# First 24 gathers of a graph layer from x, multiplied by W on TensorE, beside the making of x W

## The chip, the cores and the metric

The kernel runs on one core of a Trainium2 chip. The metric is the device time of one execution in microseconds (us); the time before is the median of three runs. The profile shows one of these executions. Its engines are TensorE (PE in the rows, PEld for its weight loads), VectorE (DVE), ScalarE (ACT), GpSimd (POOL) and SyncE (SP). SP, ACT and GpSimd issue DMAs; a row such as `SPq` or `ACTq` is the issue of one.

## The reference

Four graph layers run one after the other on 6250 nodes of 128 features, each followed by a layer norm. The graph has 206,250 edges, sorted by destination. The change touches layer 0 alone: every edge takes the row of x W at its source, times a row made from 16 edge attributes, and the sum over the edges of a destination is added to x.

```python
def _L0_gnn_ref(x, edge_index, edge_attr, W, edge_w, b):
    src, dst = (edge_index[0], edge_index[1])
    xw = x @ W
    ew = edge_attr @ edge_w
    msg = xw[src] * ew
    out = jax.ops.segment_sum(msg, dst, num_segments=x.shape[0])
    return out + b
...
x = _layernorm(x + _L0_gnn_ref(x, edge_index, edge_attr_16, L0_gnn_W, L0_gnn_edge_w, L0_gnn_b), axis=-1)
```

Layers 1 to 3 sum over the same edges without edge attributes; the kernel does that with a dense matrix of counts (the adjacency), which it makes while layer 0 runs.

## The kernel before

**Prologue.** TensorE multiplies the transposed x by W in seven turns of seven blocks of 128 nodes (L1377). ScalarE copies each turn out of the accumulators in two pieces (L1681) into one of four rooms, which lie in the memory that the gathered rows use later, and SyncE stores the room to `xw` in memory (L645). From the fifth turn on the copy waits until the room's last store has ended. Beside that VectorE finds where the edges of each pair of nodes begin: 25 reductions (L838), then the bias is copied into all of `yT` (L842) and the edges' places in their windows are made (L844). GpSimd makes constants, and one small gather (L749) that needs VectorE's first result.

**The loop** has 202 steps (n) of 1024 edges. In a step:

- GpSimd issues eight gathers (L775), each of 128 rows of `xw` of 512 bytes, 64 KB. There are four rooms for the gathered rows, so step n waits for the messages of step n - 4. From step 7 on the fifth gather waits as well for the window of step n - 2 (`s_pe`) and for the adjacency tiles made up to then (`s_amm`).
- TensorE makes the edge rows one step ahead ("edge products", L1386). VectorE multiplies them by the gathered rows as soon as all eight have landed: the message, two instructions (L984). TensorE sums the messages into a window of 64 nodes by a product with a 0/1 matrix (L1465), and VectorE adds the window to `yT` (L902).
- From step 5 on one or two tiles of the adjacency are made in a step: VectorE makes 0/1 matrices (L888, L890), TensorE multiplies them in two halves (L1438), ScalarE copies each half out (L1696), and SyncE stores the tile (L661). The edges for it come in 25 further gathers ("slots", L758), which VectorE splits in step 2 for the first time.
- From step 15 on some steps also take a job of the layers' next parts; the first of these reads x, which ScalarE loads by two DMAs (L1686, L1687), issued after the last store of x W has ended.

**After the loop** come the layers 1 to 3, mostly dense matrix products on TensorE. They start from the summed `yT`.

What sets the order: every engine runs the order in which its code is written, and waits at semaphores. On GpSimd the wait ahead of the first gather (`pool.wait_ge` on `s_in["src"]`, `s_rowxw` and `s_rowst`) is for all source numbers and for all stores of x W. On SyncE the loads at the start stand in a row: the first table, W, four pieces of the transposed x, the other weights, the source numbers, and so on.

## Time and profile before

| | |
|---|---|
| median of three runs | 2810.82 us (2810.70 to 2816.72) |
| the profiled execution | 2810.70 us, span 2808.9 us |
| TensorE busy | 2238.8 us, 80% of the span |
| VectorE busy | 1564.6 us, 56% |
| GpSimd busy | 1651.5 us, 59% |
| ScalarE busy | 498.4 us, 18% |
| TensorE's granted clock, mean | 0.809 |

Busy times are sums over stages that are limited by different things: the prologue to 32 us, the loop to about 2100 us, the dense layers behind it. In the timeline a row gives the start in us from the span's start, the duration in us, the engine, the line of the kernel, the operation, what it writes and reads, how many instructions are merged in the row (xN), and in brackets the engine's idle time ahead of it with what ended it. TensorE's clock has two levels, 1.2 and 2.4 GHz; the column PEclk shows 0.50 and 1.00 for them.

### The profile page before, as it was taken

The numbers are of one execution on the slowest core, as the hardware profiler recorded it, in microseconds if no ns is written. First come the engines' busy times: TensorE is split into PE (matmuls) and PEld (weight loads), VectorE is DVE, ScalarE is ACT, GpSimd is POOL, SyncE is SP. The second block draws the span as 40 slices with busy tenths as digits, with TensorE's granted clock in tenths as the row PEclk, the third lists the DMA queues.
The fourth block names the chain that finished last, engine by engine and source line by source line (L and its number), as shares of the span: only waits on it lengthen the run. The fifth ranks groups of instructions, "written<-read, shape, count | busy, mean of one in ns | idle before, by whom it ended". The sixth has DMA issues, their size and how long they took to land.

```text
span 2808.9 us, 35420 instructions
## 1 busy us (share of the span) xinstructions
PE 2238.8 (80%) x13074; PEld 1423.0 (51%) x13074; DVE 1564.6 (56%) x2590; ACT 498.4 (18%) x798; POOL 1651.5 (59%) x1762
## 2 busy tenths in 40 slices
PE   4677777886787767787778787777778999999995
PEld 3455555554554545555555554544444444455553
DVE  3688888788887666666667664222228111212126
ACT  1122222222222111111212111000004111111113
POOL 4777777777777777777777777777762000012222
PEclk6566777778787777787878777777679999999998
DMA  7234443445455444554545557544447787776651
GB/s 231 82 110 127 124 136 123 137 142 141 140 153 153 125 141 127 143 148 129 168 141 154 153 152 145 152 127 112 100 124 245 261 290 276 259 287 247 246 200 46
DMA packets 456701, 456.24 MB, mean 162 GB/s; under 512 B 204789, under 2 KB 402250, under 8 KB 456522
## 3 DMA queue, kind: packets, MB, share of 16 engines
q1 hardware_dynamic: 212046, 271.95, 28.3%
q0 software_dynamic: 52832, 109.16, 14.7%
q10 hardware_dynamic: 191644, 72.77, 10.6%
q8 instruction: 109, 1.79, 0.3%
q14 instruction: 70, 0.57, 0.1%
HBM read 368.61 MB, written 85.13 MB: 162 GB/s over the span
## 4 chain that ended last, share of the span: by engine, by line
PE 45%; POOL 20%; issue 11%; DMA 11%; DVE 10%; ACT 1%; DVEq 1%; SPq 1%; POOLq 0%; ACTq 0%
POOL big L775 19%; PE pb L1465 11%; DMA big<-xw,big 10%; PE pb L1569 9%; PE pb L1570 9%; PE pb L1386 6%; DVE big L984 4%; PE pb L1438 3%; PE pb L1428 2%; PE pb L1444 2%; DVE big L888 2%; DVE big L890 1%; PE pb L1587 1%; DVEq L897 1%; ACT tmp L1696 1%
## 5 line engine op out<-in xcount | busy, mean ns | idle before, releaser
L775 POOL DMA_INDIRECT big<-xw,big x1612 | 1525.8, 947 | 528.8 <-issue 496.0
L1386 PE MATMUL pb<-big 64*128 64x512 f32 x808 | 310.1, 853 | 463.1 <-DVE big L984 460.0
L984 DVE TENSOR_TENSOR big<-pb,big 128x512 f32<-128x512 f32 x404 | 259.8, 685 | 702.6 <-DMA big<-xw,big 679.7
L1465 PEld LDWEIGHTS pb<-big 128*128 128x128 f32 x3232 | 539.5, 261 | 219.0 <-issue 170.7
L1465 PE MATMUL pb<-big 128*128 128x64 f32 x3232 | 572.5, 351 | 1.4 <-DVE big L984 1.4
L1696 ACT CAST tmp<-pb 128x784 f16<-128x784 f32 x392 | 318.3, 812 | 1310.0 <-PE pb L1438 1275.5
L888 DVE TENSOR_TENSOR big<-pb,big 128x2048 f16<-128x2048 f32 x196 | 447.1, 2281 | 0.8
L890 DVE TENSOR_TENSOR big<-pb,big 128x1568 f16<-128x1568 f32 x196 | 348.4, 1778 | 0.0
L1386 PEld LDWEIGHTS pb<-big 64*128 64x128 f32 x808 | 77.1, 233 | 502.2 <-DVE big L984 490.7
L1438 PE MATMUL pb<-big 128*128 128x98 f16 x3136 | 249.0, 232 | 45.4 <-ACT tmp L1696 28.9
L1438 PEld LDWEIGHTS pb<-big 128*128 128x128 f16 x3136 | 222.0, 117 | 106.1 <-issue 47.7
L1569 PE MATMUL pb<-big,x 128*128 128x512 f16 (+1 forms) x637 | 229.7, 369 | 6.5 <-issue 6.5
L1569 PE MATMUL pb<-big,yT 128*128 128x512 f16 (+1 forms) x637 | 230.2, 368 | 3.8 <-DMA big<-at 3.8
L1570 PE MATMUL pb<-big,yT 128*128 128x512 f16 (+1 forms) x637 | 230.2, 368 | 0.0
L1570 PE MATMUL pb<-big,x 128*128 128x512 f16 (+1 forms) x637 | 229.4, 368 | 0.0
L1428 PE MATMUL pb<-big,yT 128*128 128x448 f16 x910 | 219.2, 398 | 0.0
L1444 PE MATMUL pb<-tmp,ident 128*128 128x392 f16 x784 | 215.6, 411 | 0.0
L802 POOL TENSOR_TENSOR wts<-x 128x256 f32<-128x256 f32 x24 | 16.8, 723 | 246.5 <-DVE x L1266 246.5
L790 POOL MEMSET vecs<- 128x256 f32 x1 | 0.3, 312 | 271.0 <-DVE yT L1213 271.0
L1428 PEld LDWEIGHTS pb<-big,yT 128*128 128x128 f16 x910 | 101.4, 113 | 102.0 <-issue 44.5
L855 DVE TENSOR_TENSOR big<-pb,big 128x512 f32<-128x512 f32 x202 | 137.2, 679 | 0.0
L1194 DVE SCALAR_TENSOR_TENSOR y<-pb,small,y 128x128 f32<-128x128 f32 x49 | 13.9, 344 | 182.8 <-PE pb L1587 182.8
(230 smaller groups left out, 1639.7 us busy)
## 6 DMA issues: line engine op xcount, KB each, us to landing
at<-tmp SPq DMA_DIRECT2D x196, 392.0 KB
big<-at SPq DMA_DIRECT2D x24, 3200.0 KB, 11.2
big<-at SPq DMA_DIRECT2D x24, 3072.0 KB, 19.8
big<-xw,big POOLq DMA_INDIRECT x1612
big<-at ACTq DMA_DIRECT2D x22, 896.0 KB
big<-at ACTq DMA_DIRECT2D x27, 672.0 KB
big<-in_ea SPq DMA_DIRECT2D x202, 64.0 KB
tmp<-at ACTq DMA_DIRECT2D x9, 896.0 KB
```

The source lines that it names most:

```text
L775: nc.gpsimd.indirect_dma_start(gath[:, T8 * (n % NG) + t % T8, :], None, xw_d, bass.IndirectOffsetOnAxis(ap=src_i[:, t:t + 1], axis=0)).th ...
L888: nc.vector.tensor_tensor(hot_lo[:, at_pair:at_pair + NPR, :], cols[:, 0:P].unsqueeze(1).broadcast_to([P, NPR, P]), lokeyT[:, b % 3, c:c + ...
L890: last = nc.vector.tensor_tensor(hot_key[:, at_pair:at_pair + NPR, :], cols[:, P:P + KW].unsqueeze(1).broadcast_to([P, NPR, KW]), lokeyT[: ...
L984: nc.vector.tensor_tensor(msg[:, T8 * (n % 2) + 4 * q:T8 * (n % 2) + 4 * q + 4, :], PB[:, q, :].rearrange("p (t f) -> p t f", f=D), gath[: ...
L1386: last = nc.tensor.matmul(PB[:, q, :], ea[4 * ED * q:4 * ED * q + 4 * ED, n % NG, :], edge_w[4 * ED * q:4 * ED * q + 4 * ED, 4 * q:4 * q + ...
L1428: nc.tensor.matmul(bank, parts_v[part_of][:, b0 + b, :], a_piece[:, :, b, :], start=(b == 0 and part_of == 0), stop=(b == size - 1 and par ...
L1438: last = nc.tensor.matmul(PB[:, 4 + g, i * KW:i * KW + KW], hot_lo[:, at_pair, :], hot_key[:, at_pair, :], start=True, stop=True)
L1444: last = nc.tensor.matmul(PB[:, 6, 0:NB * T8], ident16[:, :], stage[:, j % 2, :].rearrange("p (h d) -> p h d", d=SN)[:, :, g * T8:g * T8 + ...
L1465: last = nc.tensor.matmul(PB[:, 2 + n % 2, 0:WIN], msg[:, T8 * (n % 2) + t, :], hot_win[:, T8 * (n % 2) + t, :], start=(t == 0), stop=(t = ...
L1569: nc.tensor.matmul(PB[:, c, 0:n], hi[:, b, :], piece, start=(b == 0), stop=False)
L1570: last = nc.tensor.matmul(PB[:, c, 0:n], lo[:, b, :], piece, start=False, stop=(k == 2 and b == NB - 1))
L1696: nc.scalar.copy(stage[:, j % 2, :].rearrange("p (h d) -> p h d", d=SN)[:, :, c:c + 4 * GP].rearrange("p h (k i a) -> p h k i a", k=2, a=2 ...
```

## The change

Three steps of eight gathers (KX = 3) take rows of the input x instead of rows of `xw`. They need only the first 24 columns of the source numbers, which come by a DMA of their own, second in SyncE's row. The waits for all of x W and for the other source numbers move from the first gather to the first gather of step 3; the first slot gather moves from behind step 0 to behind step 2. TensorE turns the gathered rows (`turned_rows`, four tiles of 128 rows at a time), ScalarE copies the turned rows out, TensorE multiplies them by W (`rows_w`), and ScalarE copies the product back over the gathered rows; there are six such groups, all ahead of the first edge product. x W for the other steps is staged in the memory of the messages and of the adjacency's 0/1 matrices, since the gathered rows' memory is in use. VectorE waits for all stores of x W before its first message. ScalarE's load of x stands behind its new copies.

The diff, cut to what the steps need:

```diff
@@ -442,7 +445,21 @@
         POOL_ALL = 2 + 6 * 2 * NPAIR
         aggr_at, shift_at = [], []
         xT = y_room[:, 0:NB, :].rearrange("p b f -> p (b f)")
-        xwS = gath
+        key_rows = hot_key.rearrange("p t f -> p (t f)")
+        xw_rooms = [msg[:, T8 * t:T8 * t + BT, :] for t in range(2)]
+        xw_rooms += [key_rows[:, t * 2 * BT * D:(t + 1) * 2 * BT * D].bitcast(F32).rearrange("p (t f) -> p t f", f=D) for t in range(2)]
+
+        def turn_at(k):
+
+            return k + 1 if k < 2 else 2 * k
+
+        def product_at(k):
+
+            return min(2 * k + 3, 4 * KX)
+
+        turned_at = ring_at + 2 * 2 * T
+        turned_rooms = [BIG[:, turned_at + k * 2 * 4 * P:turned_at + (k + 1) * 2 * 4 * P].bitcast(F32) for k in range(2)]
+        assert turned_at + 4 * 4 * P <= 2 * CH * NB * SN
 
 
 
@@ -623,6 +640,8 @@
         @block.sync
         def _(sp):
             sp.dma_start(firstq_i, firstq_d.broadcast_to([P, QN])).then_inc(s_in["firsts"], 16)
+            with nc.allow_non_contiguous_dma(reason="24 columns, once"):
+                sp.dma_start(src_i[:, 0:KX * T8], src_d[:, 0:KX * T8]).then_inc(s_src0, 16)
             sp.dma_start(wts[:, W_L0, :], w_d[W_L0]).then_inc(s_in["w0"], 16)
             for part_of in range(4):
                 c0, c1 = XT_CUTS[part_of] * BT * P, XT_CUTS[part_of + 1] * BT * P
@@ -630,7 +649,7 @@
             sp.dma_start(wts[:, 1:7, :], w_d[1:7].rearrange("w k n -> k w n")).then_inc(s_in["w"], 16)
             with nc.allow_non_contiguous_dma(reason="128 numbers, once"):
                 sp.dma_start(bias_l0[:, :], vec_d[0, B_L0, :].rearrange("(f o) -> f o", o=1)).then_inc(s_in["w"], 16)
-            sp.dma_start(src_i, src_d).then_inc(s_in["src"], 16)
+            sp.dma_start(src_i[:, KX * T8:T], src_d[:, KX * T8:T]).then_inc(s_in["src"], 16)
             sp.dma_start(half_i, half_d.broadcast_to([P, NH])).then_inc(s_in["edges"], 16)
             sp.dma_start(dst_i, dst_d).then_inc(s_in["edges"], 16)
             sp.dma_start(win_tab[:, :], half_d).then_inc(s_in["edges"], 16)
@@ -643,7 +662,7 @@
             for t in range(NT):
                 sp.wait_ge(s_rowev, 2 * t + 2)
                 sp.dma_start(xw_d[t * BT * P:(t + 1) * BT * P, :].rearrange("(b p) f -> p b f", p=P),
-                             xwS[:, T8 * (t % 4):T8 * (t % 4) + BT, :]).then_inc(s_rowst[t % 4], 16)
+                             xw_rooms[t % 4]).then_inc(s_rowst[t % 4], 16)
                 if t == NT - 2:
                     sp.wait_ge(s_first, 2)
                     sp.dma_start(first_d.rearrange("(p b) o -> p (b o)", b=NPB), run_edge[:, :]).then_inc(s_run, 16)
@@ -758,12 +777,15 @@
                 nc.gpsimd.indirect_dma_start(slots[:, b % 2, :, :].rearrange("p e k -> p (e k)"), None, edges_d,
                                              bass.IndirectOffsetOnAxis(ap=first_edge[:, b:b + 1], axis=0)).then_inc(s_slot[b % 2], 16)
 
-            pool.wait_ge(s_in["src"], 16)
-            pool.wait_ge(s_rowxw, 2 * NT)
-            for h in range(4):
-                pool.wait_ge(s_rowst[h], 16 * ((NT + 3 - h) // 4))
+            pool.wait_ge(s_src0, 16)
             pool.sem_inc(s_seen, 1)
             for n in range(NH):
+                if n == KX:
+                    pool.wait_ge(s_in["src"], 16)
+                    pool.wait_ge(s_rowxw, 2 * NT)
+                    for h in range(4):
+                        pool.wait_ge(s_rowst[h], 16 * ((NT + 3 - h) // 4))
+                    pool.sem_inc(s_seen, 1)
                 if n >= NG:
                     pool.wait_ge(s_msg, 2 * (n - NG) + 2)
                     pool.sem_inc(s_seen, 1)
@@ -772,9 +794,9 @@
                         pool.wait_ge(s_pe, n)
                         pool.wait_ge(s_amm, 2 * made_by(n - 2))
                         pool.sem_inc(s_seen, 1)
-                    nc.gpsimd.indirect_dma_start(gath[:, T8 * (n % NG) + t % T8, :], None, xw_d,
+                    nc.gpsimd.indirect_dma_start(gath[:, T8 * (n % NG) + t % T8, :], None, x_d if n < KX else xw_d,
                                                  bass.IndirectOffsetOnAxis(ap=src_i[:, t:t + 1], axis=0)).then_inc(s_gath[n % NG], 16)
-                if n == 0:
+                if n == KX - 1:
                     slots_in(0)
                 if n + 6 in SLOTS_AT:
                     slots_in(SLOTS_AT[n + 6])
@@ -977,10 +999,15 @@
                 v.wait_ge(s_deg["col"], 4 * turn + 4)
 
             window_hot(0)
+            for h in range(4):
+                v.wait_ge(s_rowst[h], 16 * ((NT + 3 - h) // 4))
             for n in range(NH):
                 v.wait_ge(s_pe, n + 1)
-                v.wait_ge(s_gath[n % NG], 16 * T8 * (n // NG) + 16 * min(T8, ET - n * T8))
+                if n >= KX:
+                    v.wait_ge(s_gath[n % NG], 16 * T8 * (n // NG) + 16 * min(T8, ET - n * T8))
                 for q in range(2):
+                    if n < KX:
+                        v.wait_ge(s_first_act, product_at(2 * n + q))
                     nc.vector.tensor_tensor(msg[:, T8 * (n % 2) + 4 * q:T8 * (n % 2) + 4 * q + 4, :], PB[:, q, :].rearrange("p (t f) -> p t f", f=D),
                                             gath[:, T8 * (n % NG) + 4 * q:T8 * (n % NG) + 4 * q + 4, :], ALU.mult).then_inc(s_msg, 1)
                 if n + 1 < NH:
@@ -1446,7 +1473,32 @@
                 if j == NA - 1:
                     last.then_inc(s_sd, 1)
 
+            def turned_rows(k):
+                n, q = k // 2, k % 2
+                pe.wait_ge(s_gath[n], 16 * T8)
+                if k >= 2:
+                    pe.wait_ge(s_first_act, turn_at(k - 2))
+                for t in range(4):
+                    last = nc.tensor.transpose(PB[:, 4 + q, t * P:t * P + P], gath[:, T8 * n + 4 * q + t, :], ident[:, :])
+                last.then_inc(s_first_pe, 1)
+
+            def rows_w(k):
+                pe.wait_ge(s_first_act, turn_at(k))
+                if k >= 2:
+                    pe.wait_ge(s_first_act, product_at(k - 2))
+                for t in range(4):
+                    last = nc.tensor.matmul(PB[:, 2 + k % 2, t * P:t * P + P], turned_rooms[k % 2][:, t * P:t * P + P], wts[:, W_L0, :], start=True, stop=True)
+                last.then_inc(s_first_pe, 1)
+
+            pe.wait_ge(s_const, 3)
+            turned_rows(0)
+            turned_rows(1)
             pe.wait_ge(s_rowev, 2 * NT)
+            for k in range(2 * KX):
+                rows_w(k)
+                if k + 2 < 2 * KX:
+                    turned_rows(k + 2)
+            pe.wait_ge(s_first_act, 4 * KX)
             pe.wait_ge(s_tab, 3)
             edge_products(0).then_inc(s_pe, 1)
             for n in range(NH):
@@ -1678,7 +1730,22 @@
                     if t >= 4 and q == 0:
 
                         act.wait_ge(s_rowst[t % 4], 16 * (t // 4))
-                    nc.scalar.copy(xwS[:, T8 * (t % 4) + 4 * q:T8 * (t % 4) + 4 * q + nb, :], PB[:, 2 * (t % 2) + q, 0:nb * P].rearrange("p (b n) -> p b n", n=P)).then_inc(s_rowev, 1)
+                    nc.scalar.copy(xw_rooms[t % 4][:, 4 * q:4 * q + nb, :], PB[:, 2 * (t % 2) + q, 0:nb * P].rearrange("p (b n) -> p b n", n=P)).then_inc(s_rowev, 1)
+
+            def turned_out(k):
+                act.wait_ge(s_first_pe, turn_at(k))
+                if k >= 2:
+                    act.wait_ge(s_first_pe, product_at(k - 2))
+                nc.scalar.copy(turned_rooms[k % 2], PB[:, 4 + k % 2, :]).then_inc(s_first_act, 1)
+
+            turned_out(0)
+            turned_out(1)
+            for k in range(2 * KX):
+                act.wait_ge(s_first_pe, product_at(k))
+                act.wait_ge(s_first_pe, turn_at(k // 2 * 2 + 1))
+                nc.scalar.copy(gath[:, T8 * (k // 2) + 4 * (k % 2):T8 * (k // 2) + 4 * (k % 2) + 4, :], PB[:, 2 + k % 2, :].rearrange("p (t f) -> p t f", f=D)).then_inc(s_first_act, 1)
+                if k + 2 < 2 * KX:
+                    turned_out(k + 2)
 
             for h in range(4):
                 act.wait_ge(s_rowst[h], 16 * ((NT + 3 - h) // 4))
```

On GpSimd, from the small gather to the first gather of step 4. The names in brackets are the semaphores waited for: `xw_stored` and `xw_mm` are the stores and products of x W, `in_src` the source numbers. Before:

```order
L749 DMA big<-in_first,first_q_i 128x256 [waits coarse_counts]
L775 DMA big<-xw,big 128x128 [waits xw_stored2,xw_stored1,xw_stored3,xw_stored0,in_src,xw_mm]
L775 DMA big<-xw,big 128x128 x7
L758 DMA big<-in_edges,first_edge 128x256 [waits first_edges_in]
L775 DMA big<-xw,big 128x128 x16
L758 DMA big<-in_edges,first_edge 128x256
L775 DMA big<-xw,big 128x128 x8
L775 DMA big<-xw,big 128x128 [waits msg_done]
```

and with the change:

```order
L768 DMA big<-in_first,first_q_i 128x256 [waits coarse_counts]
L797 DMA big<-in_x,big 128x128 [waits first_sources_in]
L797 DMA big<-in_x,big 128x128 x23
L777 DMA big<-in_edges,first_edge 128x256 [waits first_edges_in]
L777 DMA big<-in_edges,first_edge 128x256
L797 DMA big<-xw,big 128x128 [waits xw_stored2,xw_stored1,xw_stored3,xw_stored0,in_src,xw_mm]
L797 DMA big<-xw,big 128x128 x7
L797 DMA big<-xw,big 128x128 [waits msg_done]
```

The 24 gathers of x stand where nothing waits for x W; that wait, and both slot gathers, now stand between step 2 and step 3.

On TensorE, from the last blocks of x W to the first window. `gathered0` to `gathered2` are the landings of the rows of steps 0 to 2, `first_rows_out_of_psum` counts ScalarE's new copies. Before:

```order
L1377 MATMUL pb<-wts,y 128x128 [waits xw_evac]
L1377 MATMUL pb<-wts,y 128x128 x2
L1386 MATMUL pb<-big 128x512 [waits dve_table_step,xw_evac,ea_in0,in_edge_w,in_w]
L1386 MATMUL pb<-big 128x512
L1386 MATMUL pb<-big 128x512 [waits ea_in1,msg_done]
```

and with the change, from the turn of step 2's first four tiles on:

```order
L1482 MATMUL pb<-ident,big 128x128 [waits first_rows_out_of_psum,gathered2]
L1482 MATMUL pb<-ident,big 128x128 x3
L1490 MATMUL pb<-wts,big 128x128 [waits first_rows_out_of_psum]
L1490 MATMUL pb<-wts,big 128x128 x3
L1482 MATMUL pb<-ident,big 128x128 [waits first_rows_out_of_psum,gathered2]
L1482 MATMUL pb<-ident,big 128x128 x3
L1490 MATMUL pb<-wts,big 128x128 [waits first_rows_out_of_psum]
L1490 MATMUL pb<-wts,big 128x128 x3
L1490 MATMUL pb<-wts,big 128x128 [waits first_rows_out_of_psum]
L1490 MATMUL pb<-wts,big 128x128 x3
L1413 MATMUL pb<-big 128x512 [waits ea_in0,dve_table_step,first_rows_out_of_psum]
L1413 MATMUL pb<-big 128x512
```

The first edge product, which stood right behind x W, now stands behind the products of all three steps' rows.

## Rows read from the trace of the kernel before

**Rows 1.** The page: the gathers' group (busy, mean ns, idle before); their queue.

```profile
L775 POOL DMA_INDIRECT big<-xw,big x1612 | 1525.8, 947 | 528.8 <-issue 496.0
...
q0 software_dynamic: 52832, 109.16, 14.7%
```

**Rows 2.** Timeline, GpSimd: small gather, first, step 2's last, and last gather.

```profile
6.63 1.19 POOL L749 DMA_INDIRECT big<-in_first,first_q_i  x1 [2.59 <-DVE first_q L830]
31.98 0.95 POOL L775 DMA_INDIRECT big<-xw,big  x1 [24.15 <-issue]
...
61.97 0.94 POOL L775 DMA_INDIRECT big<-xw,big  x1 [0.31 <-issue]
...
2092.78 0.94 POOL L775 DMA_INDIRECT big<-xw,big  x1 [0.30 <-issue]
```

**Rows 3.** Timeline, VectorE in the prologue: the copy into yT, the windows' places.

```profile
23.60 3.45 DVE L842 COPY yT<-bias_l 128x6336 f32<-128x6336 f32 x1
26.96 1.83 DVE L844 TENSOR_TENSOR big<-big 128x1616 f32<-128x1616 int32 x1
```

**Rows 4.** Timeline, GpSimd and VectorE in steps 6 to 8.

```profile
109.45 0.94 POOL L775 DMA_INDIRECT big<-xw,big  x1 [0.30 <-issue]
...
111.57 1.83 DVE L1005 TENSOR_TENSOR tmp<-big 128x1616 f32<-128x1616 int32 x1
111.95 2.27 POOL L775 DMA_INDIRECT big<-xw,big  x1 [0.30 <-issue]
...
123.48 1.82 DVE L1008 TENSOR_SCALAR_CACHE_REDUCE tmp<-tmp 128x1616 f32<-128x1616 f32 x1
124.51 0.94 POOL L775 DMA_INDIRECT big<-xw,big  x1 [0.30 <-issue]
```

**Rows 5.** Timeline, VectorE: messages 0, 1 and 2.

```profile
47.45 1.29 DVE L984 TENSOR_TENSOR big<-pb,big 128x512 f32<-128x512 f32 x2 [17.43 <-DMA big<-xw,big]
...
54.58 1.29 DVE L984 TENSOR_TENSOR big<-pb,big 128x512 f32<-128x512 f32 x2 [5.24 <-PE pb L1465]
...
64.64 1.29 DVE L984 TENSOR_TENSOR big<-pb,big 128x512 f32<-128x512 f32 x2 [8.05 <-DMA big<-xw,big]
```

**Rows 6.** Timeline, ScalarE and TensorE: copy, end of x W, edge product, turns.

```profile
8.14 0.59 ACT L1681 COPY big<-pb 128x512 f32<-128x512 f32 x1 [6.12 <-PE pb L1377]
...
22.83 3.36 PE L1377 MATMUL pb<-wts,y 128*128 128x128 f32 x14 [4.87 <-ACT big L1681]
...
48.80 2.08 PE L1386 MATMUL pb<-big 64*128 64x512 f32 x4 [17.53 <-DVE big L984]
...
71.46 0.64 PE L1395 MATMUL pb<-ident,tmp 128*128 128x128 f32 x2
```

**Rows 7.** Stretches: length, busy us (instructions) by engine, PEclk, DMA share, GB/s.

```profile
core 0: us, PE busy (x) PEld busy (x) DVE busy (x) ACT busy (x) POOL busy (x), PEclk, DMA share, GB/s
5.00:10.00 5.00, 3.94 (x18) 3.97 (x19) 0.68 (x4) 1.06 (x2) 1.19 (x1) 1.00 1.00 399
10.00:15.00 5.00, 5.00 (x43) 5.00 (x42) 1.97 (x10) 2.85 (x6) 0.00 (x0) 1.00 1.04 381
31.00:48.00 17.00, 0.27 (x2) 0.00 (x0) 0.55 (x1) 0.02 (x1) 12.28 (x13) 0.50 1.02 272
45.00:110.00 65.00, 39.56 (x155) 27.45 (x155) 27.84 (x74) 2.81 (x4) 49.16 (x53) 0.50 0.33 90
48.80:61.60 12.80, 11.36 (x40) 7.97 (x40) 2.55 (x5) 0.00 (x0) 9.75 (x11) 0.50 0.37 109
```

**Rows 8.** Timeline, GpSimd and TensorE in steps 22 and 23: a waiting gather, full-clock durations.

```profile
276.58 0.74 PE L1438 MATMUL pb<-big 128*128 128x98 f16 x8 [0.29 <-ACT tmp L1696]
...
278.10 0.94 POOL L775 DMA_INDIRECT big<-xw,big  x1 [2.88 <-issue]
...
278.77 1.13 PE L1386 MATMUL pb<-big 64*128 64x512 f32 x4
279.83 2.00 PE L1465 MATMUL pb<-big 128*128 128x64 f32 x16
```

More of the change, by code:

```diff
@@ L77 @@
 RING = 4
+KX = 3
 REDO_ROWS = 3 + 3 * NT
@@ L318, in build @@
         s_seen = sem("wait_over")
+        s_src0 = sem("first_sources_in")
+        s_first_pe, s_first_act = sem("first_rows_turned_or_times_w"), sem("first_rows_out_of_psum")
         s_ea = [sem(f"ea_in{h}") for h in range(NG)]
```

## The prediction

> **What bounds the kernel now.** I read the page first, then the prologue and the first steps in the timeline, one engine at a time, and last the stretches. The page's costliest group is the gather on GpSimd: 1612 of them at 947 ns, with 528.8 us of idle time ahead of them, nearly all put to "issue" [rows 1]. In the timeline they stand 1.25 us apart, 0.94 busy and 0.30 gap, from 31.98 us, where the first one starts after 24.15 us of nothing, to 2092.78 us [rows 2]. 1612 gathers and 25 slot gathers at 1.25 us are 2046 us of the 2061 between, and the idle time is 24.15, then 1611 gaps of 0.30 to 0.31, and some 13 us in waits, such as the 2.88 us at 278.10 [rows 8]. So from 32 us to 2094 GpSimd issues almost without a break; VectorE and TensorE follow it, and VectorE waits for rows to land, 8.05 us at step 2 [rows 5]. Ahead of 31.98 GpSimd does nothing after the small gather at 6.63. What follows the loop begins when the loop ends. A gather stream that is earlier by some time at step 7, and does not lose it again, ends the kernel earlier by the same time.
>
> **What is removed.** The first gather no longer needs x W in memory. It stands behind the small gather, 6.63 + 1.19, and a gap of 0.30: 8.12 instead of 31.98 [rows 2]. These 23.9 us are the ceiling, and three things take from it.
>
> **GpSimd beside VectorE.** The 24 gathers of rows of x need 23 x 1.25 + 0.94 = 29.7 us, up to 37.8. They now lie beside VectorE's prologue, a copy of 3.45 us from 23.60 and a two-operand instruction of 1.83 us to 28.79 [rows 3]. In the loop an instruction of that second kind, 1.83 us too, met a gather: that gather took 2.27 us instead of 0.94 and ended 0.82 us after VectorE's instruction [rows 4]. A reduction of 1.82 us held none (the gather beside it took 0.94 [rows 4]), so the 25 reductions ahead of the copy cost nothing. Beside such a copy no gather stands in this trace. Bounds: 1.3 us if only the two-operand instruction holds, 4.7 if one gather is held from 24.3 through both to 28.79 + 0.82. I take 3.8: 5.28 us of VectorE work at the loop's proportion, 1.33 us lost of 1.83. The 24th gather ends at 41.6.
> The Trainium skill (SBUF — State Buffer, "Who interferes with whom") speaks against the change here: a one-source copy in a mode with two ports takes the pair through which GpSimd writes descriptors, and shuts it out for its whole length. The copy at 0.54 ns a column, half the 1.13 of the instruction behind it [rows 3], would fit that mode. The same section infers that a two-operand instruction does not stop descriptors; rows 4 show one that does, and the measurement decides. By the page alone the loss would be about 3.5 us, and the sum 0.3 us lower than mine.
>
> **TensorE's new work, on the path.** Rows land 1.7 us after the last gather where loads are quiet (61.97 + 0.94, message at 64.64), and 5.8 after while x is loaded (the eighth gather ends at 31.98 + 7 x 1.25 + 0.94 = 41.67, message at 47.45) [rows 2, 5]. The load of x now starts after ScalarE's last new copy, so I take 1.7: 43.3 us. TensorE then has, in its order, four turns, four products, four turns and eight products before the first edge product. Two turns took 0.64 us; 14 instructions of x W, two to a product, took 3.36 [rows 6]. That is 1.28 + 1.92 + 1.28 + 1.92 + 1.92 = 8.3; with the last copy out (0.59 [rows 6]) and hand-overs of 0.2 it is 9.1 us. Edge product 0 starts at 52.4. What comes before that in the new chain is covered: x W ends at 26.2 [rows 6], then eight turns, a product group, and four turns, four products, four turns, four products make 10.9 us, so x W may come 6.2 us later, at 32.4, before it moves anything. That cover is for the DMA engines, which are full from 5 us to 48 [rows 7]: 24 gathers of 64 KB at this queue's rate (109.16 MB in 14.7% of the span [rows 1], 264 GB/s) are 6.0 us of all 16.
>
> **Three steps that start late and run faster.** Message 0 comes at 52.4 + 2.08 [rows 6] + 0.06 = 54.5 us; before it came at 47.45. But three steps of rows are then ready, and the steps run at what TensorE and VectorE need, not at the gathers' 10 us. That is the row where the second message waited for TensorE and not for a DMA: 54.58 - 47.45 = 7.13 us [rows 5]. This is at 1.2 GHz: the granted clock is 0.50 from 45 to 110 us, and also from 48.80 to 61.60, where TensorE was busy for 11.36 of 12.80 us [rows 7]. Message 5 is at 54.5 + 5 x 7.13 = 90.2. GpSimd, after two slot gathers, ends step 3 at 54.4, waits for message 0 (its end at 55.9), and from 56.2 would reach the fifth gather of step 7 at 91.2. There it must wait for window 5 and for the first adjacency tile: 90.2 + 7.1 + 0.74 (half a tile) = 98.0, and a gather starts 0.8 after such a wait (276.58 + 0.74 to 278.10 [rows 8]): **98.8 us instead of 109.45** [rows 4], 10.6 us earlier. The wait at the fifth gather of step 8, 10 us on, is met: message 6 at 97.3, its window and half tile by 105.2. From there gathers pace again as before, 10.6 us earlier.
>
> **What costs nothing.** The new rooms for x W add no instruction; VectorE's wait for the stores, which GpSimd waited for until 31.98, is over long before message 0. ScalarE's twelve copies of 0.59 stand between TensorE's groups and are counted where one is last. Behind them on ScalarE is the load of x, some 21 us later, now beside the landings of steps 3 and 4: with 5.8 us these come at 60 and 72, and are needed at 75.9 and 83.1. Its first reader is step 15, beyond 180 us at 10 us a step. SyncE issues one small load more ahead of W and the transposed x (an issue of about 0.5 us, inside the cover of 6.2). The slots are gathered two steps later, before step 3, and are first used in VectorE's step 2, at 69.
>
> **Sum.** The profiled execution took 2810.70 us (span 2808.9), the median of the runs 2810.82. 2810.8 - 10.6 = **2800.2 us**. With the unknowns at their ends: a hold of 1.3 gives 2797.7; a hold of 4.7 and a landing of 5.8 give 2805.2.
>
> **Rivals.**
> *TensorE's clock rises.* The new tail is 8.3 us of nearly unbroken TensorE work. The stream of x W ran 18 instructions in 3.94 us (0.22 each) and then 43 in 5.00 (0.12 each) [rows 7], so unbroken work from 6 us on did bring 2.4 GHz. Against it stands the 0.50 of 48.80 to 61.60. If the clock is full from edge product 0 on for ten us, that product takes 1.13 instead of 2.08, and in two steps product and window take 1.13 + 2.00 [rows 8] instead of 5.75: 6.2 us less, 2794.0, and with a hold of 1.3 some 2791.5.
> The Trainium skill (TensorE: Matmul & The Clock Gate, "Part 4: PE-mode transpose") says that turns do not count as work for the clock in the way that matmuls do, which speaks against this rival; no run here shows it.
> *The lead is given back.* GpSimd waits for TensorE's tiles at some steps behind 7 (step 23 [rows 8]). If TensorE paces the loop there, GpSimd's lead only makes it wait longer: 2806 to 2811. Against it: those waits are some 13 us of 2061, and where VectorE waits for rows its work moves with the gathers.
> *Slower.* 24 gathers among full DMA engines slow the stores of x W, for which ScalarE's copies wait, and all behind them. This decides where x W ends after 42.9 instead of 26.2: edge product 0 then starts 20.0 later (10.9 + 9.1), at 62.9, and 10.5 us are gone; each us more costs one. With x W at 48.5 it is 2816. Against it: the 6.0 us of engine time above.
> That the change does not do what it says is hardly left: 24 gathers of x stand first in GpSimd's order, and only late source numbers could hold them.
>
> **How the numbers follow.** Forecast 0.45, higher clock 0.32, lead given back 0.13, slower 0.10. A measurement here can tell about 0.2%, 5.6 us, from no change. Of the first two some lies under 2791, of the last two most above 2806, together no more than 2 in 10: the range is 2791 to 2806. Faster 0.78 (the first two and a little of the third), same 0.13, slower 0.09.
>
> **What would show it.** First gather at 8.1; one or two gathers of 2 to 4 us beside the copy into yT; the 24th ended by 42; message 0 at 54.5 with 0.50 granted from 45 to 98 (1.00 after 50 is the rival); steps of 7.1 us; one idle time of some 7 us before the fifth gather of step 7, at 98.8; the last gather at 2082. Wrong if message 0 is after 60, if the shift at step 30 is not that at step 8, or if a step with all its rows landed takes 9 us.

## The result

The changed kernel took 2796.45 us, median of four runs (2790.66 to 2799.63), beside 2813.77 us for the kernel before on the same chip, four runs (2810.70 to 2817.47). The ratio is 0.9932, 95% interval 0.9918 to 0.9946: 19 us by the ratio, 17.3 by the medians. The forecast was 2800.2 us (2791 to 2806). The profiled execution took 2790.66 us with a span of 2788.1, 20.8 less than the span before. So the direction and the range held, and the gain was 1.6 to 1.8 times the 10.6 us of the forecast.

The gathers first. These are rows of the timeline of GpSimd, with the two rows of VectorE that stand beside the long gathers:

```profile
7.81 0.95 POOL L797 DMA_INDIRECT big<-in_x,big  x1 [0.31 <-issue]
...
22.81 3.90 POOL L797 DMA_INDIRECT big<-in_x,big  x1 [0.30 <-issue]
23.14 3.45 DVE L864 COPY yT<-bias_l 128x6336 f32<-128x6336 f32 x1
26.51 1.84 DVE L866 TENSOR_TENSOR big<-big 128x1616 f32<-128x1616 int32 x1
27.02 2.14 POOL L797 DMA_INDIRECT big<-in_x,big  x1 [0.30 <-issue]
...
40.70 0.94 POOL L797 DMA_INDIRECT big<-in_x,big  x1 [0.30 <-issue]
...
90.36 0.94 POOL L797 DMA_INDIRECT big<-xw,big  x1 [1.30 <-PE pb L1465]
...
2070.19 0.95 POOL L797 DMA_INDIRECT big<-xw,big  x1 [0.30 <-issue]
```

The first gather starts at 7.81 instead of 31.98 [rows 2], 24.2 us earlier. Two of the 24 gathers of x are long, 3.90 and 2.14 instead of 0.94: 4.2 us lost. At step 7 the fifth gather waits 1.30 - 0.30 = 1.0 us for the adjacency tile and stands at 90.36 instead of 109.45 [rows 4], 19.1 earlier. The last gather stands at 2070.19 instead of 2092.78, 22.6 earlier, so in this trace the lead is kept to the loop's end (in the other traces it moves on the way, see below); 22.6 - 20.8 = 1.8 us of it are gone behind the loop.

The timeline of TensorE (with ScalarE's last copy): the end of x W, then from the last rows of x to edge product 0; and VectorE's messages 0, 1, 2, 3 and 5:

```profile
25.56 3.36 PE L1404 MATMUL pb<-wts,y 128*128 128x128 f32 x14 [7.51 <-ACT big L1733]
...
43.21 0.66 PE L1482 MATMUL pb<-ident,big 128*128 128x128 f32 x4 [1.87 <-DMA big<-in_x,big]
43.71 1.18 PE L1490 MATMUL pb<-wts,big 128*128 128x128 f32 x8
44.68 1.06 PE L1482 MATMUL pb<-ident,big 128*128 128x128 f32 x4
45.54 3.09 PE L1490 MATMUL pb<-wts,big 128*128 128x128 f32 x16
48.66 0.58 ACT L1746 COPY big<-pb 128x512 f32<-128x512 f32 x1 [0.59 <-PE pb L1490]
49.30 1.13 PE L1413 MATMUL pb<-big 64*128 64x512 f32 x4 [0.68 <-ACT big L1746]
50.67 1.29 DVE L1011 TENSOR_TENSOR big<-pb,big 128x512 f32<-128x512 f32 x2 [21.11 <-PE pb L1413]
55.11 1.29 DVE L1011 TENSOR_TENSOR big<-pb,big 128x512 f32<-128x512 f32 x2 [2.55 <-PE pb L1517]
60.67 1.29 DVE L1011 TENSOR_TENSOR big<-pb,big 128x512 f32<-128x512 f32 x2 [3.54 <-PE pb L1517]
67.78 1.29 DVE L1011 TENSOR_TENSOR big<-pb,big 128x512 f32<-128x512 f32 x2 [3.10 <-issue]
...
81.91 1.29 DVE L1011 TENSOR_TENSOR big<-pb,big 128x512 f32<-128x512 f32 x2 [1.15 <-PE pb L1517]
```

Message 0 is later than before (50.67 against 47.45 [rows 5]), message 5 is 13.9 us earlier (81.91 against 95.83), since the first steps run at TensorE's pace of 4.4, 5.6 and then 7.1 us instead of the gathers' 10. Message 5 in the trace before, waiting for rows to land:

```profile
95.83 1.29 DVE L984 TENSOR_TENSOR big<-pb,big 128x512 f32<-128x512 f32 x2 [4.08 <-DMA big<-xw,big]
```

Four turns took 0.66 us in one row and 1.06 in another, and edge product 0 took 1.13, the duration of rows 8, not the 2.08 of rows 6. The stretches say why. Behind the five engines' busy times (instructions in brackets) stand the granted clock, the DMA share and GB/s:

```profile
40.00:45.00 5.00, 3.13 (x21) 2.94 (x21) 0.00 (x0) 1.62 (x4) 3.78 (x5) 0.84 0.23 68
45.00:50.00 5.00, 4.33 (x24) 3.74 (x22) 0.00 (x0) 2.27 (x5) 3.78 (x5) 0.71 0.24 66
50.00:55.00 5.00, 3.41 (x23) 2.16 (x20) 1.89 (x3) 0.00 (x0) 3.78 (x5) 1.00 0.89 234
55.00:60.00 5.00, 3.62 (x20) 2.79 (x19) 2.01 (x4) 0.00 (x0) 3.78 (x5) 0.82 1.06 294
60.00:95.00 35.00, 29.51 (x121) 20.67 (x122) 24.93 (x67) 2.81 (x4) 25.78 (x28) 0.50 0.43 123
45.00:110.00 65.00, 51.04 (x254) 36.60 (x252) 41.31 (x90) 8.32 (x13) 48.45 (x52) 0.63 0.49 138
```

From the last turns to the second step TensorE had 2.4 GHz for the larger part of the time, and 1.2 GHz from 60 us to 95. Before, the stretch from 45 to 110 stood at 0.50 [rows 7].

### The profile page after: what moved, and what is told of

It reads as the page before. It is cut to its first block, busy times and chain, and to the rows that moved or that the text cites. A ratio compares the mean times of both kernels' runs of the same rounds, so it can differ in the third digit from the quotient of the medians.

```text
span 2788.1 us, 35600 instructions
## 1 busy us (share of the span) xinstructions
PE 2243.8 (80%) x13146; PEld 1428.2 (51%) x13146; DVE 1563.7 (56%) x2590; ACT 505.3 (18%) x810; POOL 1653.1 (59%) x1762
## 3 DMA queue, kind: packets, MB, share of 16 engines
q0 software_dynamic: 52832, 109.16, 14.6%
q10 hardware_dynamic: 191644, 72.77, 10.7%
q8 instruction: 109, 1.79, 0.3%
## 4 chain that ended last, share of the span: by engine, by line
PE 47%; POOL 18%; DVE 11%; DMA 11%; issue 11%; DVEq 1%; ACT 1%; POOLq 0%; ACTq 0%
POOL big L797 18%; PE pb L1517 12%; DMA big<-xw,big 10%; PE pb L1621 9%; PE pb L1622 9%; PE pb L1413 7%; DVE big L1011 4%; PE pb L1465 3%; DVE big L910 2%; PE pb L1455 2%; DVE big L912 2%; PE pb L1471 1%; DVEq L919 1%; PE pb L1639 1%; PE pb L1551 1%
## 5 line engine op out<-in xcount | busy, mean ns | idle before, releaser
L797 POOL DMA_INDIRECT big<-xw,big x1588 | 1500.8, 945 | 497.5 <-issue 463.6
L1517 PEld LDWEIGHTS pb<-big 128*128 128x128 f32 x3232 | 531.9, 257 | 219.7 <-issue 180.5
L1517 PE MATMUL pb<-big 128*128 128x64 f32 x3232 | 564.7, 348 | 1.4 <-DVE big L1011 1.4
L1221 DVE SCALAR_TENSOR_TENSOR y<-pb,small,y 128x128 f32<-128x128 f32 x49 | 13.9, 344 | 182.9 <-PE pb L1639 182.9
```

The source lines that it names most:

```text
L797: nc.gpsimd.indirect_dma_start(gath[:, T8 * (n % NG) + t % T8, :], None, x_d if n < KX else xw_d, bass.IndirectOffsetOnAxis(ap=src_i[:, t: ...
L1517: last = nc.tensor.matmul(PB[:, 2 + n % 2, 0:WIN], msg[:, T8 * (n % 2) + t, :], hot_win[:, T8 * (n % 2) + t, :], start=(t == 0), stop=(t = ...
```

## The experiments

Two theories went in. Theory A: the chain of the forecast is right (message 0, then six steps of TensorE, then the gather of step 7), and only TensorE's durations were put too long. Theory B: TensorE's chain no longer matters at step 7, and GpSimd's own stream alone sets the time. Each kernel is the changed one with the edit that is shown. The table gives medians, the ratio to the kernel before that ran beside it, with its interval, and three times from each trace: message 0, message 5, and the fifth gather of step 7 with the idle time ahead of it (0.30 is the usual gap).

| kernel | median (before), us | ratio | message 0 | message 5 | fifth gather, step 7 (idle) |
|---|---|---|---|---|---|
| after | 2796.45 (2813.77) | 0.9932 [0.9918, 0.9946] | 50.67 | 81.91 | 90.36 (1.30) |
| again | 2794.90 (2815.12) | 0.9933 [0.9919, 0.9947] | 50.84 | 82.28 | 90.73 (2.40) |
| late_first | 2812.82 (2815.12) | 0.9988 [0.9979, 0.9997] | 62.31 | 97.69 | 106.14 (7.04) |
| kx2 | 2802.84 (2815.12) | 0.9962 [0.9949, 0.9976] | 43.81 | 81.16 | 94.82 (0.30) |
| no_product | 2793.30 (2815.12) | 0.9927 [0.9914, 0.9941] | 46.00 | 81.36 | 89.81 (0.56) |
| warm | 2789.83 (2810.15) | 0.9933 [0.9918, 0.9948] | 51.05 | 75.82 | 89.42 (0.30) |
| nohold | 2792.45 (2810.15) | 0.9932 [0.9916, 0.9948] | 47.34 | 80.08 | 88.53 (2.62) |
| kx4 | 2807.81 (2810.15) | 0.9986 [0.9977, 0.9994] | 63.78 | 97.46 | 105.91 (5.35) |
| kx2_slots | 2796.53 (2810.15) | 0.9944 [0.9929, 0.9959] | 42.25 | 78.42 | 92.03 (0.30) |
| nohold_warm | 2785.85 (2809.99) | 0.9913 [0.9898, 0.9928] | 48.23 | 72.54 | 86.02 (0.30) |
| again_2 | 2794.10 (2809.99) | 0.9940 [0.9926, 0.9953] | 49.66 | 82.30 | 90.75 (2.56) |

Wherever the gather waited (idle above 0.30), it stands 8.45 us behind message 5, in all seven rows. The forecast's figure for that piece was 98.8 - 90.2 = 8.6.

The times follow the lead at step 7, which is 109.45 less the start in the last column. By the ratio late_first gains 3.4 us with a lead of 3.3, after 19.1 with 19.1, and nohold_warm 24.4 with 23.4; kx2 is furthest off, 10.7 us with 14.6. So a gather that is earlier at step 7 does end the kernel earlier by about as much, to within 4 us.

### The changed kernel again

No edit.

> The changed kernel once more, unaltered. Theory A (clock): the gain beyond the forecast is TensorE's clock; where it is full in the row products and the first steps, GpSimd sets the pace from step 3 on, and the fifth gather of step 7 starts near 90 us; where it is half, TensorE's chain sets it, near 99. So this profile has that gather between 90 and 99, later the more of 43 to 60 us is at 0.50, and the runs spread over several us. Theory B (cover): TensorE's chain is never what that gather waits for; it starts at 89.5 to 90.5 at any clock, and the spread comes from elsewhere.

2794.90 us. Message 0 came at 50.84, and the second step took 5.8 us, since the clock fell in it, as in the first trace. In the third copy, again_2 below, it fell sooner, at the start of that step.

### Edge product 0 later

```diff
             pe.wait_ge(s_first_act, 4 * KX)
+            pe.wait_ge(s_gath[KX], 16 * T8)
             pe.wait_ge(s_tab, 3)
```

> One wait added: TensorE makes edge product 0 only when the rows of step 3 have landed too, near 55.3 us instead of 49.3, and idles meanwhile. Theory A: TensorE's chain has no slack at step 7 (0.98 us of waiting there already), so the delay comes through in full, and the idle TensorE falls back to 0.50: message 0 at 57.5, steps of 7.13, fifth gather of step 7 at 57.5 + 35.7 + 7.1 + 0.7 + 0.8 = 101.8, some 11 us later than 90.4; total 2804 to 2808. If the clock is full in the first steps, some 6 us later. Theory B: that gather does not depend on edge product 0; no change beyond 1 to 2 us.

The timeline of VectorE and GpSimd in late_first, and its stretch from 60 to 95:

```profile
62.31 1.29 DVE L1011 TENSOR_TENSOR big<-pb,big 128x512 f32<-128x512 f32 x2 [32.75 <-PE pb L1413]
64.38 0.95 POOL L797 DMA_INDIRECT big<-xw,big  x1 [10.21 <-DVE big L1011]
69.37 1.29 DVE L1011 TENSOR_TENSOR big<-pb,big 128x512 f32<-128x512 f32 x2 [5.18 <-PE pb L1518]
...
97.69 1.29 DVE L1011 TENSOR_TENSOR big<-pb,big 128x512 f32<-128x512 f32 x2 [1.15 <-PE pb L1518]
106.14 0.95 POOL L797 DMA_INDIRECT big<-xw,big  x1 [7.04 <-PE pb L1465]
...
60.00:95.00 35.00, 28.27 (x95) 18.22 (x96) 14.07 (x32) 0.37 (x1) 23.30 (x25) 0.50 0.36 100
```

Message 0 is 11.6 us later than in the changed kernel, the gather of step 7 is 15.8 later, and the ratio is 0.9988: some 3 us are left of the gain. The expectation had edge product 0 at 55.3; it started at 60.0, 5.8 us after the last gather of step 3 had ended (53.22 + 0.95), while ScalarE's load of x was on its way. This is the forecast's longer landing, 5.8 us beside that load; by it message 0 is 4.8 us later than the 57.5 expected, and the median lies above the 2804 to 2808 expected. GpSimd, which had the same early start, stood 9.9 us at step 4 for message 0 and 6.7 at step 7 for the tile. So theory B falls: TensorE's chain does set the time when it is late. Here the clock stood at 0.50 from 60 to 95, and the steps from message 0 to message 5 took 35.38 us, 7.08 each, against the forecast's 7.13. From message 0 on, the forecast's chain at 1.2 GHz is therefore right, from a start that a wait, and not TensorE's work, made late.

### TensorE's new work left out

```diff
...
-            pe.wait_ge(s_const, 3)
-            turned_rows(0)
-            turned_rows(1)
             pe.wait_ge(s_rowev, 2 * NT)
-            for k in range(2 * KX):
-                rows_w(k)
-                if k + 2 < 2 * KX:
-                    turned_rows(k + 2)
-            pe.wait_ge(s_first_act, 4 * KX)
+            pe.wait_ge(s_gath[KX - 1], 16 * T8)
...
```

ScalarE's twelve copies go with it. The messages of the three steps are made from the raw rows of x, for which VectorE waits instead, so these steps' values are not the layer's; the load of x waits for edge product 0.

> Left out: the turns, the products by W and ScalarE's twelve copies for the first three steps; the messages of these steps are made from the raw rows of x. Edge product 0 waits for the rows of step 2, as the row products did, and the load of x waits for edge product 0. Edge product 0 at 43.3 instead of 49.3. Theory A: the wait at step 7 goes, the fifth gather starts at 89.4, and the total is 1 us below the best run of the change, and below its median by 4 to 6, since the clock no longer decides. Theory B: as the change, within 1 us.

The timeline of TensorE in no_product from the end of x W to the second edge product, and its stretch from 25 to 90:

```profile
25.41 3.36 PE L1402 MATMUL pb<-wts,y 128*128 128x128 f32 x14 [7.29 <-ACT big L1724]
43.69 2.08 PE L1411 MATMUL pb<-big 64*128 64x512 f32 x4 [14.92 <-DMA big<-in_x,big]
47.34 2.08 PE L1411 MATMUL pb<-big 64*128 64x512 f32 x4 [1.58 <-DVE big L1009]
...
25.00:90.00 65.00, 41.25 (x156) 29.00 (x157) 28.86 (x76) 4.79 (x10) 49.50 (x51) 0.50 0.61 165
```

Here the clock stood at 0.50 from 25 us to 90, the edge product took 2.08, and message 5 came 81.36 - 46.00 = 35.36 us behind message 0. This is the forecast's pace again, now from an early start. And it shows what the new work costs: it put message 0 back by 50.67 - 46.00 = 4.7 us and the gather of step 7 by only 0.55, because the clock was up behind that work and the next two steps were shorter (4.4 and 5.6 us instead of 7.06 each). In time the two kernels cannot be told apart (0.9927, and 0.9932 to 0.9940 for the changed kernel).

### TensorE kept busy in steps 0 to 5

```diff
                 for j in MADE[n][:1]:
                     a_products(j, 0)
+                if n < 6:
+                    for _ in range(10):
+                        nc.tensor.matmul(PB[:, 6, 0:P], ident16[:, :], ident16[:, :], start=True, stop=True)
                 pe.wait_ge(s_msg, 2 * n + 2)
```

> The changed kernel with ten products of the identity by itself (128 columns, into an accumulator that nobody reads) on TensorE in each of steps 0 to 5, where it waits for the message: 0.5 to 1.1 us of a wait of 1.3. Theory A (clock): the granted clock stays at 1.00 after 50 us, the steps with landed rows take 4.5 us instead of 7.1, the wait at the fifth gather of step 7 (0.98 and 2.08 us in two profiles) goes, and that gather starts near 89; total 1 to 2 us below the change. Theory B: the clock in these steps is of no account; no change. If the clock does not rise, the steps stay at 7.1 to 7.4 and the total may be 1 us above.

Stretches of warm:

```profile
50.00:55.00 5.00, 4.08 (x32) 2.41 (x28) 1.89 (x3) 0.00 (x0) 3.78 (x5) 1.00 0.80 215
55.00:60.00 5.00, 4.18 (x40) 3.24 (x39) 2.08 (x5) 0.00 (x0) 3.78 (x5) 1.00 1.07 296
60.00:65.00 5.00, 4.18 (x41) 3.18 (x37) 4.29 (x16) 0.37 (x1) 3.78 (x5) 1.00 1.06 291
...
70.00:75.00 5.00, 3.06 (x20) 2.16 (x20) 5.00 (x5) 0.00 (x0) 3.78 (x5) 0.98 0.25 71
75.00:95.00 20.00, 16.88 (x91) 12.45 (x92) 15.82 (x44) 3.25 (x4) 15.43 (x16) 0.50 0.26 73
```

With 60 products that compute nothing the clock stayed up to 75 us, the first three steps took 4.4 to 4.5 us, the next two waited for their own rows to land (4.9 and 6.5 us), and the wait at step 7 vanished; the gather came 0.9 us sooner than in the changed kernel. From there GpSimd's stream alone sets the pace, as theory B says, but only because TensorE is ahead. A gain over the changed kernel is not resolved: the ratio is 0.9933, and the changed kernel's three are 0.9932 to 0.9940.

### The copy into yT moved off VectorE

```diff
             nc.vector.tensor_scalar(run_edge[:, :], before_16[:, :], first_q[:, 0:1], float(2 * FE), ALU.add, ALU.mult).then_inc(s_first, 1)
-            v.wait_ge(s_in["w"], 32)
-            nc.vector.tensor_copy(yT[:, :], bias_l0[:, 0:1].broadcast_to([P, YW]))
...
                     act.wait_ge(s_rowxw, 2 * t + q + 1)
+                    if t == 4 and q == 0:
+                        act.wait_ge(s_in["w"], 32)
+                        nc.scalar.copy(yT[:, :], bias_l0[:, 0:1].broadcast_to([P, YW]))
```

> The copy of the bias into yT (3.45 us, 6336 columns) moves from VectorE to ScalarE, where it stands behind the eighth copy of x W, in a wait of 9.5 us for the stores. Two gathers were held beside VectorE's copy and the instruction behind it, 4.15 us together. Theory H (hold): only the two-operand instruction is left, a loss of about 1.2; the 24th gather ends near 38.7 instead of 41.6, edge product 0 starts near 46.3, the fifth gather of step 7 near 87.5, and the total is 3 us below the change. Rival: edge product 0 then waits for x W or for TensorE's other groups instead, or the slots' first gather waits for its places (near 37), and the total falls by less than 1 us.

The timeline of ScalarE, VectorE and GpSimd in nohold:

```profile
16.29 5.47 ACT L1730 COPY yT<-bias_l 128x6336 f32<-128x6336 f32 x1 [1.68 <-DMA bias_l<-in_vec]
...
23.21 1.83 DVE L864 TENSOR_TENSOR big<-big 128x1616 f32<-128x1616 int32 x1
24.07 1.79 POOL L797 DMA_INDIRECT big<-in_x,big  x1 [0.30 <-issue]
26.17 0.95 POOL L797 DMA_INDIRECT big<-in_x,big  x1 [0.30 <-issue]
...
88.53 0.94 POOL L797 DMA_INDIRECT big<-xw,big  x1 [2.62 <-PE pb L1463]
```

The gather of 3.90 is gone, so VectorE's copy was what held it; the loss is 0.85 instead of 4.2. ScalarE's copy of 5.47 us held no gather. GpSimd is 3.2 us further ahead at step 3 (41.19 against 44.44), but at step 7 only 1.8, because it now waits 2.3 us for TensorE there: a gain on one chain stops at the other. The clock had also fallen sooner: the second step took 7.06 us. In the ratio nothing can be seen (0.9932).

### Both of these edits

The two diffs above, together.

> Both edits together: the copy into yT on ScalarE, and ten products of the identity by itself on TensorE in each of steps 0 to 5. With the copy alone GpSimd's lead at step 3 grew from 20.1 to 23.3 us, but 2.30 us went again in the wait at the fifth gather of step 7, with TensorE at 1.2 GHz from 58 us on; with the products alone that wait went. Theory A: together the fifth gather of step 7 starts near 86.3 without a wait, 23 us earlier than in the kernel before, and the total is 3 to 4 us below the change. Theory B: the lead is lost elsewhere before the loop ends; as the change.

Stretches of nohold_warm, and its fifth gather of step 7:

```profile
45.00:50.00 5.00, 3.40 (x27) 2.15 (x27) 1.77 (x3) 1.17 (x3) 3.78 (x5) 1.00 0.48 136
...
65.00:70.00 5.00, 4.18 (x37) 3.25 (x36) 3.96 (x5) 0.00 (x0) 3.78 (x5) 1.00 0.27 72
70.00:75.00 5.00, 3.43 (x26) 2.44 (x25) 4.42 (x7) 0.81 (x1) 3.78 (x5) 0.66 0.26 69
...
86.02 0.94 POOL L797 DMA_INDIRECT big<-xw,big  x1 [0.30 <-issue]
```

Now neither chain waits for the other at step 7, and the gather stands 4.7 us ahead of again_2, which ran beside it. The median is 2785.85 us, 24.1 below the kernel before and 8.2 below again_2 (2782.89 to 2786.70 against 2789.30 to 2797.74). This is the lowest median of the study, and the kernel is faster than both kernels of the case; from no_product and warm, which ran beside other runs, the intervals of the ratios do not separate it. In the two traces the lead over again_2 grows from 4.7 us at step 7 to 10.7 at the last gather, and the spans differ by 11.2. The growth goes with fewer waits of GpSimd behind step 7: idle time beyond the gap of 0.30, counted where it is over 0.05 us, is 9.2 us in sum here and 16.1 in again_2. Why they are fewer was not isolated, and since copies of one kernel differ in this too (see what stays open), only the 4.7 us are shown to come from the two edits.

### The changed kernel a third time

No edit.

> The changed kernel once more, beside the version with both edits on the same chip. From the two profiles taken so far: message 0 at 50.7 to 50.8, two steps of 4.4 to 5.7 us and then steps of 7.1, the fifth gather of step 7 at 90.4 to 90.7 with a wait of 1 to 2 us; total 17 to 20 us below the kernel before. Theory A: a profile in which the clock falls earlier has this gather later by 2.6 us a step; theory B: it stands at 89.5 to 90.5 whatever the clock.

2794.10 us, ratio 0.9940. In this trace the clock was up earlier (0.97 from 45 to 50 us, message 0 at 49.66) and down earlier: the second step took 61.06 - 54.09 = 6.97 us instead of 5.6. The two cancel, and message 5 came out at 82.30, as in again.

### Two steps from x, or four

```diff
-KX = 3
+KX = 2
```

> Two steps of rows from x instead of three (KX = 2). GpSimd: the 16th gather ends at 31.7, then it waits for x W and the first slots, near 34.4, so step 3 begins near 47 instead of 44.4: its lead is 2.5 us smaller. TensorE: the last rows land at 33.3 instead of 43.2, edge product 0 at 40 to 42 instead of 49.3. Theory A: no wait at step 7 at either clock; fifth gather of step 7 at 91.5 to 92; the total is 2 us above the best run of the change but without its spread, median equal or up to 2 us lower. Theory B: only GpSimd's lead counts, 2.5 us slower than the change in every run.

With the slot gathers left where the code of the change puts them for KX = 2, they come too soon. The timeline of GpSimd in kx2:

```profile
37.42 0.94 POOL L777 DMA_INDIRECT big<-in_edges,first_edge  x1 [5.67 <-DMA first_edge<-first_edges]
```

They wait 5.4 us for the edges' places, which VectorE and two small DMAs make. Steps 3 to 30 are 14.6 to 14.8 us ahead instead of 19 to 20, with no wait at step 7, and the ratio is 0.9962. In kx2_slots the slot gathers stay behind step 2:

```diff
-KX = 3
+KX = 2
...
-                if n == KX - 1:
+                if n == 2:
                     slots_in(0)
```

> Two steps of rows from x, as in the run with KX = 2, but the first slot gather behind step 2 instead of step 1. There GpSimd idled 5.67 us before the slot gather, for the places of the slots, and only then went on. If that wait is what the run with KX = 2 lost, step 2's gathers now start when x W is in memory, near 35.9 instead of 38.7, and the total is 1.5 to 3 us below it, still 4 us above three steps. If x W in memory was the limit there, no change.

The timeline of GpSimd in kx2_slots, first gather of step 2:

```profile
34.62 0.94 POOL L797 DMA_INDIRECT big<-xw,big  x1 [2.92 <-DMA xw<-big]
```

Now the wait is for the last store of x W, 2.6 us, and the lead at step 7 is 17.4, where three steps have 18.7 to 19.1. So two steps are too few for x W to be in memory in time, and three are enough: in the changed kernel step 3 starts at 44.44 with no idle time but the gap. In time the two cannot be told apart (0.9944, and 0.9932 to 0.9940). Four are too many:

```diff
-KX = 3
+KX = 4
...
-                if n == KX - 1:
+                if n == 2:
                     slots_in(0)
```

> Four steps of rows from x (KX = 4); the first slot gather stays behind step 2. GpSimd's lead is not larger than with three, since nothing waits for x W there. The last rows land near 56 instead of 43.2, edge product 0 starts at 62 to 65. Theory A: the delay comes through at step 7: message 0 near 64, that gather at 64 + 39.7 to 43.8, so 104 to 108; total 2806 to 2812, 12 to 17 us above the change. Theory B: as the change.

The timeline of TensorE in kx4 from the last rows of x on, and its stretches:

```profile
55.93 1.12 PE L1482 MATMUL pb<-ident,big 128*128 128x128 f32 x4 [8.23 <-DMA big<-in_x,big]
...
59.40 2.33 PE L1490 MATMUL pb<-wts,big 128*128 128x128 f32 x16
...
62.40 1.13 PE L1413 MATMUL pb<-big 64*128 64x512 f32 x4 [0.68 <-ACT big L1746]
...
55.00:60.00 5.00, 4.07 (x19) 4.08 (x20) 0.00 (x0) 1.53 (x3) 0.00 (x0) 0.50 0.04 9
60.00:65.00 5.00, 2.86 (x19) 1.84 (x17) 1.22 (x3) 1.40 (x4) 0.00 (x0) 0.98 0.23 51
```

The fourth step's rows land at 55.93 only, and the same tail of turns, products and copies (6.5 us) stands behind them: message 0 comes at 63.78. GpSimd waits 11.3 us for it at step 4 and 5.05 at step 7, and the ratio is 0.9986. This is late_first by another way, with the same 8.45 us between message 5 and the gather. It also shows the clock once more: the tail began at 0.50 after 8.23 us without work, and behind it edge product 0 ran at full clock (1.13), while in late_first and no_product, where TensorE had stood idle ahead of it, it took 2.08.

## Why the prediction was right, and where it was too small

**The time, in the range by some luck.** The lead was forecast at little more than half of what it became. The median lies well inside the range in part because the four runs of the kernel before have a median 3 us above the three that the forecast started from (2813.77 and 2810.82); 19 us off 2810.8 is 2791.7, just above the lower end of 2791.

**First gather, 8.1:** 7.81. Right.

**The hold beside VectorE, 3.8 us, one or two gathers of 2 to 4 us:** 2.96 + 1.20 = 4.2 us, gathers of 3.90 and 2.14, and nohold shows the cause of the larger part. The reductions ahead of the copy held nothing. Right, and near in size; that the 24th gather ended at 41.64 (forecast 41.6) is luck, since a start 0.3 us earlier and a hold 0.4 us longer cancel.
The Trainium skill (SBUF — State Buffer, "Who interferes with whom") says that a one-source copy in a mode with two ports shuts GpSimd out for its whole length. The trace agrees on the length: the gather that had begun 0.33 us ahead of the copy ended 0.12 after it (26.71 against 26.59); the mode itself no row shows. The same section's inference that a two-operand instruction does not stop descriptors is again not borne out: the gather beside L866 took 2.14, and in nohold, with the copy moved, 1.79; both ended 0.8 us after VectorE's instruction.

**x W may end as late as 32.4:** it ended at 25.56 + 3.36 = 28.9. Right. The rival "slower" needed 42.9 and did not happen, though ScalarE's copies did wait longer for stores than before.

**Rows land 1.7 us after the last gather, at 43.3:** TensorE's turns start at 43.21, 1.6 us after it. Right.

**TensorE's new work, 9.1 us to edge product 0, and steps of 7.13 us:** this step failed, in the size of its terms. Four turns, four products (two instructions each), four turns, eight products, the copy and the hand-over (the tail) took 49.30 - 43.21 = 6.1 us instead of 9.1, for two reasons. Part of them ran at 2.4 GHz, and they were priced from rows at 1.2. And the sum was too long at 1.2 GHz as well: it added up durations of rows, but a row of TensorE begins before the row ahead of it has ended (43.21 + 0.66 is 43.87, and the next begins at 43.71). In kx4, at a clock of 0.50, the first three groups took 59.40 - 55.93 = 3.47 us, where the sum has 1.28 + 1.92 + 1.28 = 4.48. So about 1 us of the 3 is counting, and the clock is most of the rest; no run has the whole tail at 1.2 GHz. With the clock up, edge product 0 took 1.13 instead of 2.08, and the first two steps 4.4 and 5.6 instead of 7.13. Against the forecast message 0 is 3.8 us earlier and message 5 is 90.2 - 81.9 = 8.3 earlier. The piece behind that was right: 8.45 us instead of 8.6. So the fifth gather of step 7 is at 90.4 instead of 98.8, and these 8.4 us are the difference between the forecast's lead of 10.6 and the 19.1 measured.
The mechanism behind message 0 stands as it was written. With the clock down throughout (no_product, late_first) the steps take 7.07 us, and a late message 0 gives the wait of some 7 us that was forecast (6.7 in late_first).

**The rival "TensorE's clock rises"**, at 0.32, is what happened. Its price of 6.2 us counted the first edge product and two steps, but not the tail ahead of them. The weighing failed at one row: the 0.50 of 48.80 to 61.60, with TensorE busy 11.36 of 12.80 us [rows 7], was taken as evidence for how a nearly unbroken stretch of new work would run. It did not show that; 3.13 and 4.33 us busy of 5 stood at 0.84 and 0.71 in the new kernel, and 1.00 followed. The rival's own reading was no better: it takes the faster instructions after 10 us of the prologue for a rise to 2.4 GHz, but its rows show a granted clock of 1.00 in both stretches [rows 7], and what slowed the first 18 instructions no row shows.
The Trainium skill (TensorE: Matmul & The Clock Gate, "Part 4: PE-mode transpose") says that turns do not count for the clock as matmuls do. Without turns and products the clock stayed at 0.50 and with them it rose, but no run has the one without the other, so the rule is neither confirmed nor refuted here.

**The rival "the lead is given back"** did not happen: the lead was 19.7 us at step 8 and 22.6 at the last gather. GpSimd's waits behind step 7, counted as above, were 12.6 us in sum (13.8 before).

**GpSimd is then nearly the limit.** Once TensorE is that much sooner, the lead is 24.2 for the first gather, less 4.2 for the hold, less 1.0 for the wait at step 7: 19.0, where 19.1 was measured.

**What stays open.** Copies of the changed kernel run from 2789 to 2800 us, and the traces show where it arises. In its three traces the fifth gather of step 7 stands within 0.4 us, and 717.8 to 718.1 us lie between the last gather and the end; the 4.4 us by which their spans differ (2787.9 to 2792.3) come in the loop between. From step 7 to the last gather the lead went from 19.1 to 22.6 us in the first trace and from 18.7 to 18.3 in again_2; it went from 20.9 to 17.5 in nohold and from 20.0 to 24.8 in warm. The sum of GpSimd's waits there was 12.6 us in the first trace and 16.1 in again_2. What decides these waits was not isolated, and it hides gains of a few us in the total. Nor was it isolated which of TensorE's instructions raise the clock, or why it falls at the start of the second step in one trace and later in it in another.

## What to carry to other kernels

Where two engines' chains meet at one wait, work out when each arrives, for both levels of TensorE's clock: a gain on one chain stops where the other arrives. Each alone, nohold and warm moved the gather of step 7 by 1.8 and 0.9 us, and the two together by 4.3 to 4.7. New TensorE work on the path can pay for part of itself where the clock is up behind it, as here, so price it at both levels, don't take the level from a stretch with other instructions in it, and measure from start to start, since rows overlap. When a step is prepared from raw input to start a stream earlier, take as many steps as the slower path needs to be ready and no more; here two waited for x W (which the total does not resolve), four made GpSimd wait for the first message, and three did neither.

## What was not expected of the hardware

Behind some 6 us of turns and products the granted clock was 1.00 until after the first step (50 to 55 us), and with ten small products more in each step, 0.73 us of work, it was 0.98 to 1.00 until 75; without any of them it was 0.50 from 25 to 90.

A copy on VectorE held a gather of GpSimd to 0.12 us after its own end, a two-operand instruction to 0.8 us after its own; the same copy on ScalarE, at 5.47 instead of 3.45 us, held none.
